# Layers 0 to 2 of a four-layer block: phases behind barriers against one interleaved order of attention and feed-forward steps

## The chip, the cores and the metric

The kernel runs on one core of one Trainium2 chip. The metric is the device time of one execution in microseconds; the median of three runs of the kernel before is 2029.81 us (2028.09 to 2031.36). Names of engines: PE is the matrix engine (TensorE), DVE is VectorE, ACT is ScalarE, POOL is GpSimd, SP issues most DMAs.

## The reference

Input x is (2, 1024, 256), a context is (2, 154, 256), and all arithmetic is float32. Four layers, each a cross-attention and a feed-forward part, both added to x after a layer norm:

```python
    x = x + _L0_xattn_ref(_layernorm(x, axis=-1), ctx_1024, ...)   # 16 heads of 16, softmax over 154 positions
    x = x + _L0_ffn_ref(_layernorm(x, axis=-1), ...)     # ternary weights 256->1024->256, relu squared
    x = x + _L1_xattn_ref(_layernorm(x, axis=-1), ctx_1024, ...)
    x = x + _L1_ffn_ref(_layernorm(x, axis=-1), ...)     # product keys: 4 heads x 8 of 4096 table rows, plus a gated MLP
    x = x + _L2_xattn_ref(_layernorm(x, axis=-1), ctx_1024, ...)   # with rotary positions
    x = x + _L2_ffn_ref(_layernorm(x, axis=-1), ...)     # 8 experts, 2 taken, plus a shared one; gate and up, then down
    x = x + _L3_xattn_ref(_layernorm(x, axis=-1), ctx_1024, ...)   # autocorrelation instead of softmax
    x = x + _L3_ffn_ref(_layernorm(x, axis=-1), ...)     # 8 linear experts, 2 taken
```

The part of layer 1 that matters most here: for each of the 2048 tokens, 32 rows of a table are fetched, each with a 256-wide half for a dot product with the normed token and a 256-wide half that is added to x, weighted:

```python
        de = down_embed[indices]
        ue = up_embed[indices]
        ew = jnp.einsum('btd,bthkd->bthk', hidden_states, de)
        ew = jax.nn.silu(ew) * jax.nn.softmax(scores, axis=-1)
        experts_states = jnp.einsum('bthk,bthkd->btd', ew, ue)
```

## The kernel before

Tokens are handled in 4 chunks of 512 (four tiles of 128 partitions). `schedule()` lists phases: the keys and values of a layer (`kv`), then for layer 0 the attention of all four chunks, the preparation of the ternary weights (`tern`) and the four feed-forward chunks; for layers 1 and 2 the attention and the feed-forward part of chunk 0, then of chunk 1, and so on; layer 3 follows. Every engine runs the phases in this order. A phase begins on each engine with `enter`, which waits until the other two compute engines have left the phase before, and ends with `leave` (a drain). Phases share one buffer (`bufA`) and all PSUM banks.

An attention chunk has these steps. In the first pass, 12 units of up to 6 heads (of 16 per tile) are multiplied on PE (L495) and their row maxima taken on DVE (L1199, L1202, L1203), with three pairs of PSUM banks. The maxima are turned on PE (L500), copied by ACT and sent by DMA as one more row of the queries. In the second pass, scores of 4 heads at a time go to PSUM (L523, L529), ACT takes the exponentials two heads at a time (L866, L868), PE weighs the values (L510, L513). Then the result is turned (L543), divided on DVE (L1222, L1223), turned again (L548) and projected (L553). The queries of the next chunk are projected ahead (`stack`: L454), cut into three bf16 parts on DVE (L1131 to L1133), written to DRAM, and read back by SP in another layout (L1577) once the second pass no longer needs the old ones.

The layer norm of the next phase is `front`: DVE takes statistics and, with a square root from ACT, normalises (L1108 to L1123), PE turns (L443), ACT copies. ffn0 has 8 hidden tiles (L597) and 4 output tiles (L606); ffn1 has the similarities and their top 8 (L624, L1285, L1289), gate and up (L634), the choice of the 32 rows of each token (`sums` to `prob`, L1298 to L1332) and the output (L652 onwards is ffn2's); ffn2 has 10 tiles of gate and up (L663, four matmuls each, in two alternating pairs of banks) and 36 output tiles (L675).

The gather of layer 1 is cut into 128 groups of 4 fetches, 32 groups for each chunk. POOL issues the fetches (L1539, 256 KB each) into a ring of `RING = 20` row buffers, which is five groups: group g waits until group g-5 has been added. DVE computes the dots (L1043), ACT a tanh (L817), DVE the weights (L1055, L1059) and the additions (L1048). A call for group g finishes group g-1: it holds the additions of g-1 between the dots of g. A table gives the places of the groups in the phases of layers 1 and 2, over all of them up to the third ffn2:

```python
STEPS = dict(kv=(2, 0, 4), attn1=(1, 3, 2, 0, 4, 0, 1), attn2=(0, 2, 3, 0, 2, 1, 1), ffn1=(2, 0, 0, 1, 0, 0, 2),
             ffn2=(2, (1, 1, 1, 0, 1, 1, 1, 1, 1, 0), 0, 4, 2))
```

Of the kernel before, what the change touches and what calls it, by code (L numbers as in the profile page):

```python
# [9 lines left out]
P = 128  # L18
STOP = None
B, T, D = 2, 1024, 256  # L20
S = 154
H, DH = 16, 16
KT = D // P
# [15 lines left out]
RING, GRP = 20, 4  # L39
NG = PH * TOPK // GRP  # L40

# [8 lines left out]


STEPS = dict(kv=(2, 0, 4), attn1=(1, 3, 2, 0, 4, 0, 1), attn2=(0, 2, 3, 0, 2, 1, 1), ffn1=(2, 0, 0, 1, 0, 0, 2),
             ffn2=(2, (1, 1, 1, 0, 1, 1, 1, 1, 1, 0), 0, 4, 2))

TERN_ROWS = {1: range(0, 4), 2: range(4, 8), 3: range(8, 10)}


ATTN_PACK = dict(wq=KT * D, wk=KT * D, wv=KT * D, wo=KT * D, bq=2, bk=2, bv=D, bo=D)
# [3 lines left out]
FFN2_PACK = dict(gate=KT * E2, gu=KT * M2 * 2 * P, down=M2 * D)  # L62
# [3 lines left out]
ROPE_PACK = dict(cos=T, sin=T)  # L66
# [9 lines left out]

def schedule():

    out = [("kv", 0, 0)] + [("attn", 0, c) for c in range(NCH)] + [("tern", 0, 0)]

    out += [("ffn0", 0, c) for c in range(NCH - 1)] + [("kv", 1, 0), ("ffn0", 0, NCH - 1)]
    for layer in (1, 2):
        for c in range(NCH):
            out.append(("attn", layer, c))
            if layer == 1 and c == NCH - 1:
                out.append(("kv", 2, 0))
            out.append((f"ffn{layer}", layer, c))  # L90
    out.append(("kv3", 3, 0))
    for b in range(B):
        out += [("q3", b, 2 * b), ("q3", b, 2 * b + 1), ("corr", b, 0)]
    out += [("out3", b, 0) for b in range(B)]
    out += [("ffn3", 3, c) for c in range(NCH)]
    return out


def build(nc, io, stop=None):
    phases = schedule()[:stop]  # L100
    fronts = [n for n, (kind, _, _) in enumerate(phases) if kind in ("attn", "ffn0", "ffn1", "ffn2", "q3", "ffn3")]
    front_of = {n: f for f, n in enumerate(fronts)}

    def instance(n):

        return sum(p[0] == phases[n][0] for p in phases[:n])

    def next_front(n):

        f = sum(m <= n for m in fronts)  # L110
        if f >= len(fronts):
            return None
        m = fronts[f]
        kind, b, _ = phases[n]
        if phases[m][0] == "ffn3" and phases[m - 1][0] == "out3":
            return f if kind == "out3" and b == 1 else None

        return f if n == (fronts[f - 1] if f else 0) else None

    def is_tail(n):  # L120

        f = next_front(n)
        return f is not None and phases[fronts[f]][2] == phases[n][2]

    def stack_of(n):

        return n + 1 if n + 1 < len(phases) and phases[n + 1][0] == "attn" else None

    def stacks_before(f):

        return sum(phases[m][0] == "attn" for m in fronts[:f])

    ctx = ExitStack()
    with ctx:
# [8 lines left out]
        xg = [sb(f"xg{i}", [P, TI, D]) for i in range(3)]  # L143
        xt = sb("xt", [P, KT, CH])
        stats = sb("stats", [P, TI, 6])
        mv = sb("mv", [P, TI, 2])
        vare, stdev, newton, rstd = (sb(s, [P, TI]) for s in ("vare", "stdev", "newton", "rstd"))
# [7 lines left out]
        RN, (LC, LN) = columns(ROPE_PACK)[1], columns(LATE_PACK)  # L155
        const = sb("const", [P, KN])
        ctxt = sb("ctxt", [P, KT, B * S])
        wattn = sb("wattn", [P, max(AN, CN)])
        wf = sb("wf", [P, max(4096, F1N, F2N, F3N)])
        bufA = sb("bufA", [P, 8832])  # L160
        bufB = sb("bufB", [P, 10240])
        ringb = sb("ring", [P, RING * 2 * D])
# [1604 lines left out]
```

## Time and profile before

| what | value |
|---|---|
| median of three runs | 2029.81 us |
| span of the profiled execution | 2025.4 us |
| what lies around the span (median less span) | 4.4 us |
| layers 0 to 2 | 0 to 1675 us |
| layer 3 | 1675 to 2025.4 us |
| PE, DVE, ACT, POOL busy, of the span | 69%, 62%, 20%, 26% |
| 128 groups of the gather | from 571 to about 1516 us |

The profiled execution has no device time of its own in the profile beside its span, so the difference to the median stands for what lies around it. Busy times of one engine's instructions overlap a little at their edges, so that a sum of durations is longer than the time in which they run; where it matters, start-to-start times are used.

### The profile page before, as it was taken

How to read it: one execution, taken by the hardware profiler on the slowest of the kernel's cores; microseconds unless marked ns; L12 is line 12 of the kernel's file. 1: busy time of each engine (PE TensorE's matmuls, PEld its weight loads, DVE VectorE, ACT ScalarE, POOL GpSimd, SP SyncE). 2: the span in 40 equal slices, each digit the busy share in tenths (PEclk: the TensorE clock that was granted, in tenths of full speed). 3: DMA queues.
4: the chain of work that ended last, by engine and by line, in shares of the span. 5: the costliest groups of instructions: out<-in, count | busy, mean ns of one | idle time of the engine just before them, and what ended most of it. 6: DMA issues, size and time to landing. Idle time of an engine off the chain costs nothing.

```text
span 2025.4 us, 16984 instructions
## 1 busy us (share of the span) xinstructions
PE 1400.9 (69%) x5070; PEld 728.6 (36%) x5070; DVE 1255.7 (62%) x4181; ACT 415.0 (20%) x711; POOL 533.8 (26%) x560
## 2 busy tenths in 40 slices
PE   4566689976736556465627657837737788898998
PEld 2233346543312323222313233323414354344544
DVE  3445533433858878886887888878877244321675
ACT  1323341113113122131204203212210411100110
POOL 1000000000057246254426745753740000011000
PEclk8777789988958867786857877867877899999999
DMA  6433300250198468558686996996863102120000
GB/s 137 116 37 53 52 26 1 29 92 12 31 188 185 90 147 193 102 140 194 133 192 174 193 166 154 191 187 120 195 138 52 44 0 68 34 66 27 11 11 21
DMA packets 101196, 202.63 MB, mean 100 GB/s; under 512 B 27568, under 2 KB 65328, under 8 KB 99952
## 3 DMA queue, kind: packets, MB, share of 16 engines
q0 software_dynamic: 40960, 134.25, 29.8%
q1 hardware_dynamic: 60144, 67.30, 17.9%
q8 instruction: 40, 0.66, 0.1%
q14 instruction: 52, 0.43, 0.1%
HBM read 185.58 MB, written 15.73 MB: 99 GB/s over the span
## 4 chain that ended last, share of the span: by engine, by line
PE 39%; DVE 26%; DMA 17%; POOL 7%; issue 5%; ACT 3%; SPq 1%; ACTq 0%; DVEq 0%
DMA bufB<-scr_queries 8%; POOL ring L1539 7%; DVE m L1199 5%; PE psum L693 4%; DMA ring<-in_table,rowid 3%; PE psum L752 3%; DVE x_sb L1048 3%; PE psum L597 3%; PE psum L763 3%; DMA scr_queries<-bufB 2%; PE psum L523 2%; DVE ring L1043 2%; PE psum L634 2%; PE psum L606 2%; PE psum L663 2%
## 5 line engine op out<-in xcount | busy, mean ns | idle before, releaser
L1539 POOL DMA_INDIRECT ring<-in_table,rowid x512 | 508.9, 994 | 764.5 <-DVE prob L1332 329.7
L495 PE MATMUL psum<-bufB 112*128 112x154 bf16 x768 | 109.5, 316 | 224.9 <-DMA bufB<-scr_queries 184.2
L1048 DVE SCALAR_TENSOR_TENSOR x_sb<-ring,ew,x_sb 128x256 f32<-128x256 f32 x512 | 246.5, 481 | 5.0
L1043 DVE CUSTOM_DVE_ANT_0 ring<-xg,ring 128x256 f32<-128x256 f32 x512 | 212.8, 416 | 13.8 <-DMA ring<-in_table,rowid 13.8
L495 PEld LDWEIGHTS psum<-bufB 112*128 112x128 bf16 x768 | 78.6, 132 | 257.3 <-issue 191.0
L1525 POOL TENSOR_TENSOR x_sb<-x_sb,wattn 128x256 f32<-128x256 f32 x32 | 22.0, 721 | 539.8 <-ACTq L276 286.9
L1199 DVE TENSOR_REDUCE m<-psum 128x6 f32<-128x924 f32 x96 | 103.0, 1115 | 86.9 <-PE psum L495 82.0
L663 PE MATMUL psum<-xt,wf 128*128 128x512 f32 x320 | 148.4, 619 | 10.2 <-DVE bufA L1354 9.0
L1127 DVE TENSOR_TENSOR x_sb<-x_sb,psum 128x256 f32<-128x256 f32 x128 | 50.3, 418 | 125.4 <-PE psum L606 45.6
L817 ACT ACTIVATE thalf<-dots 128x4 f32<-128x4 f32 x128 | 26.2, 205 | 452.8 <-DVE dots L1043 452.1
L693 PE MATMUL psum<-wf,xt 128*128 128x512 f32 x256 | 114.3, 603 | 1.1 <-DVE x_sb L1425 1.0
L675 PE MATMUL psum<-wf,bufA 128*128 128x256 f32 x320 | 84.3, 426 | 42.4 <-DVE x_sb L1365 42.4
L523 PE MATMUL psum<-bufB 113*128 113x512 bf16 x192 | 68.1, 486 | 46.1 <-DMA bufB<-mt 40.2
L866 ACT ACTIVATE bufA<-psum 128x1024 f32<-128x1024 f32 x96 | 93.2, 1029 | 31.6 <-PE psum L523 31.5
L443 PE MATMUL psum<-const,xa 128*128 128x128 f32 x224 | 39.2, 333 | 83.5 <-DVE xa L1123 83.5
L663 PEld LDWEIGHTS psum<-xt,wf 128*128 128x128 f32 x320 | 61.8, 198 | 93.7 <-issue 70.6
L675 PEld LDWEIGHTS psum<-wf,bufA 128*128 128x128 f32 x320 | 64.4, 212 | 63.2 <-DVE x_sb L1365 51.0
L1055 DVE SCALAR_TENSOR_TENSOR ew<-dots,prob 128x4 f32<-128x4 f32 x128 | 20.4, 159 | 99.2 <-ACT thalf L817 55.7
L1425 DVE SCALAR_TENSOR_TENSOR x_sb<-psum,bufA,x_sb 128x256 f32<-128x256 f32 x128 | 61.6, 484 | 31.6 <-PE psum L693 27.1
L763 PE MATMUL psum<-bufA,bufB 128*128 128x512 f32 x160 | 71.7, 610 | 5.8 <-DMA bufA<-scr_roll 4.6
L1365 DVE SCALAR_TENSOR_TENSOR x_sb<-psum,bufA,x_sb 128x256 f32<-128x256 f32 x128 | 61.8, 483 | 16.6 <-PE psum L675 5.3
L1108 DVE BATCH_NORM_STATS2 stats<-x_sb 128x6 f32<-128x256 f32 x128 | 44.9, 413 | 43.7 <-ACTq L276 36.5
(225 smaller groups left out, 2252.8 us busy)
## 6 DMA issues: line engine op xcount, KB each, us to landing
bufB<-scr_queries SPq DMA_DIRECT2D x84, 256.0 KB, 10.0
scr_queries<-bufB SPq DMA_DIRECT2D x12, 768.0 KB, 3.7
ring<-in_table,rowid POOLq DMA_INDIRECT x512, 5.8
wf<-in_ffn SPq DMA_DIRECT2D x1, 3848.0 KB, 21.9
wattn<-in_attn SPq DMA_DIRECT2D x3, 1282.0 KB, 7.6
bufB<-scr_keys SPq DMA_DIRECT2D x42, 80.0 KB, 5.2
ring<-in_ffn SPq DMA_DIRECT2D x1, 2696.5 KB, 22.2
bufA<-scr_roll SPq DMA_DIRECT2D x4, 592.0 KB
```

The source lines that it names most:

```text
L495: ins = mm(psum[:, pair + z, at:at + S], queries[0:MROW, h, i * P:(i + 1) * P], keys(b)[0:MROW, h, 0:S], start=True, stop=True)
L523: ins = mm(bank(2 * a + z), keys(b)[0:MROW + 1, 4 * G + 2 * a + z, 0:P], queries[0:MROW + 1, 4 * G + 2 * a + z, :], start=True, stop=True)
L663: ins = mm(bank(2 * (m % 2) + r), gu[:, kt, m, r, :], x[:, kt, :], start=kt == 0, stop=kt == KT - 1)
L675: ins = mm(psum[:, y % 5, 0:D], hm2[:, m, i * P:(i + 1) * P], down[:, m, :], start=m == ms[0], stop=m == ms[-1])
L693: ins = mm(bank(y % 4), x[:, kt, i * P:(i + 1) * P], w3("we")[:, kt, e * 512:(e + 1) * 512], start=kt == 0, stop=kt == KT - 1)
L763: ins = mm(bank(2 * g + N), vst(b, g)[:, u, :], roll(2 * b + g)[:, at:at + 512], start=u == 0, stop=u == U - 1)
L866: act(p[:, 2 * a:2 * a + 2, :], psum[:, 2 * a:2 * a + 2, :], ACT.Exp).then_inc(at_ex, 1)
L1043: return eng.tensor_tensor_reduce(row, xg[c % 3][:, i, :], row, 1.0, 0.0, ALU.mult, ALU.add, dots[:, g % 4, j:j + 1])
L1048: return stt(x, ring[:, GRP * (g % (RING // GRP)) + j, D:2 * D], ew[:, g % 4, j:j + 1], x, ALU.mult, ALU.add)
L1199: eng.reduce_max(m4[:, i, h0:h1].rearrange("p (a b) -> p a b", a=2), psum[:, pair:pair + 2, 0:3 * S].rearrange("p a (b s) -> p a b s", b=3 ...
L1365: ins = add_x(c, i, src) if e == 8 else stt(x_sb[:, c * TI + i, :], src, comb2[0][:, i, e:e + 1], x_sb[:, c * TI + i, :], ALU.mult, ALU.add)
L1539: eng.indirect_dma_start(ring[:, s * GRP + j, :], None, io["table"], bass.IndirectOffsetOnAxis(ap=rowid[c % 3][:, at + j:at + j + 1], axis ...
```

## The change

The phases of layers 0 to 2 are replaced by a list of small items, which each engine walks through; what an engine has no part in, it skips. There is no barrier until layer 3; every buffer has its own semaphores. In each of 13 slots the attention items of one chunk are interleaved with the feed-forward items of the chunk before, by weights written beside them. The list's items: `p1` is a unit of the first pass, `s` half a group of the second pass, `w` the weighing, `t`, `o`, `y` the way back, `N` and `X` the two parts of a layer norm (for attention "a" and feed-forward "f"), `Q` the projection of queries, `L` their load, `g` one group of the gather.

PSUM is split: banks 0 to 3 belong to attention (first pass: two pairs instead of three; second pass: two single banks, one for the rest, one for the values), 4 and 5 to norms, queries and keys, 6 and 7 to the feed-forward part. So ffn0 has two banks for hidden tiles instead of four, and gate and up of ffn1 and ffn2 use the one pair 6 and 7. Exponentials are taken one head at a time. Keys and values are made per batch. The normalising multiplication moves from DVE to ACT. Similarities of ffn1 use only the non-zero half of the keys. The ring has `RING = 12` buffers, which is three groups, and the 128 groups are spread over slots 6 to 9 alone, 32 in each, evenly by number of items. SBUF for weights, norms and probabilities is cut anew, so that both halves of a slot fit.

```diff
-RING, GRP = 20, 4
+RING, GRP = 12, 4
+SLOTS = RING // GRP
...
+def ffn_items(layer, c):
+    if layer == 0:
+        out = [(1.75, ("h0", c, m)) for m in range(8)] + [(3.4, ("y0", c, i)) for i in range(TI)]
+    elif layer == 1:
+        out = [(3.5, ("q1", c))]
+        for i in range(TI):
+            out += [(1.0, ("sm1", c, i)), (3.5, ("gu1", c, i))]
+        out += [(0.1, ("tk1", c))] + [(1.8, ("y1", c, i)) for i in range(TI)]
+    else:
+        out = [(1.5, ("lg2", c))] + [(3.5, ("gu2", c, m)) for m in range(M2)]
+        out += [(0.5, ("y2", c, i, e)) for i in range(TI) for e in range(9)]
+    return out
...
+GATHER_PER_SLOT = {6: 32, 7: 32, 8: 32, 9: 32}
+CUTS = (0.22, 0.34, 0.42, 0.66, 0.86)
...
+        if a:
+            first, scores, back = attention_items(*a)
+            items += merged(first[:3], rest)
+            if f:
+                items.append((1.5, ("X", "f") + f))
+            if nxt:
+                items.append((0.0, ("N", "a") + nxt))
...
+            items += merged(first[3:9], ffn[0])
+            if nxt:
+                items += [(1.5, ("X", "a") + nxt)] + ffn[1] + [(3.6, ("Q",) + nxt)]
...
+            items += first[9:] + ffn[2] + merged(scores, ffn[3])
...
+            items += merged(back, ffn[4])
+            items.append((0.0, ("N", "f") + a))
...
+        order = [x for _, x in items]
+        n = GATHER_PER_SLOT.get(s, 0)
+        for z in range(n):
+            at = [q for q, x in enumerate(order) if x[0] != "g"]
+            order.insert(at[(2 * z + 1) * len(at) // (2 * n)], ("g",))
...
+            def gate2(c, m):
+                if m == 0:
+                    eng.wait_ge(f2_sc, c + 1)
+                else:
+                    eng.wait_ge(f2_hm, M2 * c + m)
...
-                if g >= RING // GRP:
-                    eng.wait_ge(f1_acc, g - RING // GRP + 1)
+                if g >= SLOTS:
+                    eng.wait_ge(f1_acc, g - SLOTS + 1)
```

What stood on PE at the first pass of chunk 1 of layer 0 (L495 is the first pass, L500 turns the maxima, L523 and L529 are scores, L443 turns a normed chunk):

```order
L495 MATMUL psum<-bufB 128x154 x64
L500 MATMUL psum<-const,m 16x128 x4
L523 MATMUL psum<-bufB 128x512 x4
L529 MATMUL psum<-bufB 32x512 x4
L443 MATMUL psum<-const,xa 128x128 x8
```

What stands there now (L595 is the first pass, L704 a hidden tile of ffn0 for chunk 0 with two matmuls each, L545 turns a normed chunk, L555 projects the next queries, L603 turns the maxima):

```order
L595 MATMUL psum<-bufB 128x154 x10
L545 MATMUL psum<-const,xa 128x128 x8
L595 MATMUL psum<-bufB 128x154 x6
L704 MATMUL psum<-xtf,wf 128x512 x2
L595 MATMUL psum<-bufB 128x154 x6
L704 MATMUL psum<-xtf,wf 128x512 x2
L595 MATMUL psum<-bufB 128x154 x10
```

The feed-forward tiles, the two norms and the queries have moved between the units of the first pass, whose maxima DVE takes.

On ACT, in the second pass of chunk 3 of layer 1, before (L817 is the tanh of a group, L866 and L868 are exponentials, L858 unloads the values):

```order
L866 ACTIVATE bufA<-psum 128x1024 x2
L868 ACTIVATE bufA<-psum,const 128x512
L817 ACTIVATE thalf<-dots 128x4
L866 ACTIVATE bufA<-psum 128x1024 x2
L868 ACTIVATE bufA<-psum,const 128x512
L858 ACTIVATE bufA<-psum 128x512
L817 ACTIVATE thalf<-dots 128x4 x2
```

The same pass of the same chunk now (L915 is the tanh, L978 and L983 are exponentials, L987 unloads, L1019 is the silu of ffn1 for chunk 2):

```order
L983 ACTIVATE bufR<-psum,const 128x512
L1019 ACT_TABLE_LOAD
L1019 ACTIVATE bufR<-psum 128x512
L915 ACTIVATE thalf<-dots 128x4
L978 ACT_TABLE_LOAD
L978 ACTIVATE bufR<-psum 128x512 x2
L987 ACTIVATE bufR<-psum 128x512
L915 ACTIVATE thalf<-dots 128x4
L978 ACTIVATE bufR<-psum 128x512 x2
L983 ACTIVATE bufR<-psum,const 128x512
```

Silu stands between exponentials, with a load of a function table ahead of it and one behind it, and the tanh of a group stands behind every second or third item. In the whole program ACT has 94 table loads now and had 60.

## Rows read from the trace of the kernel before

**Rows 1.** Stages: length, busy PE, PEld, DVE, ACT, POOL, clock, DMA share, GB/s.
```profile
324.20:354.30 30.10, 28.93 (x104) 19.01 (x105) 11.05 (x29) 5.85 (x11) 0.00 (x0) 1.00 0.00 1
452.70:501.00 48.30, 34.60 (x188) 16.57 (x188) 18.67 (x42) 16.84 (x22) 0.00 (x0) 0.82 0.09 37
571.00:1516.00 945.00, 549.22 (x1996) 279.18 (x1996) 771.07 (x2916) 201.22 (x375) 497.39 (x501) 0.75 0.76 162
1600.00:1675.00 75.00, 63.90 (x192) 38.06 (x192) 33.04 (x100) 12.81 (x20) 0.00 (x0) 0.89 0.08 29
1675.00:2025.40 350.40, 323.05 (x888) 153.68 (x888) 160.49 (x443) 39.15 (x74) 10.98 (x16) 0.99 0.12 34
0.00:1675.00 1675.00, 1077.89 (x4182) 574.88 (x4182) 1095.24 (x3739) 375.86 (x637) 522.79 (x544) 0.79 0.55 114
```

**Rows 2.** Who waited for whom, 0 to 1675 us; total, times, longest.
```profile
POOL ring L1539 <- DVE x_sb L1048: 290.6, 38, 32.5
...
PE psum L495 <- DMA bufB<-scr_queries: 184.2, 11, 30.6
...
DVE ew L1055 <- ACT thalf L817: 55.7, 21, 8.7
...
DVE ew L1055 <- DMA ring<-in_table,rowid: 39.4, 24, 3.2
```

**Rows 3.** PE in order of time; start, us, line, tiles, idle before.
```profile
120.04 4.80 PE L495 MATMUL psum<-bufB 112*128 112x154 bf16 x32 [9.55 <-DMA bufB<-scr_queries]
...
133.32 1.02 PE L500 MATMUL psum<-const,m 128*16 128x128 f32 x4 [2.37 <-DVEq L1205]
137.31 1.86 PE L523 MATMUL psum<-bufB 113*128 113x512 bf16 x4 [2.96 <-DMA bufB<-mt]
...
145.10 3.70 PE L454 MATMUL psum<-xt,wattn 128*128 128x512 f32 x8
...
159.23 1.97 PE L543 MATMUL psum<-const,bufA 128*128 128x128 f32 x16
...
324.25 13.97 PE L597 MATMUL psum<-xt,wf 128*128 128x512 f32 x32 [0.61 <-DVEq L276]
...
1609.87 36.26 PE L663 MATMUL psum<-xt,wf 128*128 128x512 f32 x80
...
1653.68 20.50 PE L675 MATMUL psum<-wf,bufA 128*128 128x256 f32 x80
```

**Rows 4.** DVE's pieces: norm, top 8 of a tile, row choice first, split, choice rest.
```profile
504.90:508.10 3.20, 3.17 (x4) 1.52 (x5) 2.62 (x13) 0.21 (x1) 0.00 (x0) 0.50 0.02 5
514.20:518.20 4.00, 4.00 (x10) 1.71 (x9) 3.91 (x24) 0.00 (x0) 0.00 (x0) 1.00 0.01 2
536.30:543.40 7.10, 6.63 (x23) 4.36 (x24) 7.02 (x52) 4.32 (x7) 0.00 (x0) 1.00 0.00 0
543.40:546.50 3.10, 3.10 (x16) 2.74 (x15) 3.00 (x3) 0.00 (x0) 0.00 (x0) 1.00 0.01 3
546.50:555.80 9.30, 0.87 (x5) 0.42 (x3) 9.03 (x17) 0.00 (x0) 0.00 (x0) 0.78 0.79 151
```

**Rows 5.** One group on DVE, from its first to its last instruction.
```profile
592.60 0.16 DVE L1055 SCALAR_TENSOR_TENSOR ew<-dots,prob 128x4 f32<-128x4 f32 x1 [0.23 <-DVE m L1203]
...
594.93 1.00 DVE L1048 SCALAR_TENSOR_TENSOR x_sb<-ring,ew,x_sb 128x256 f32<-128x256 f32 x2
```

**Rows 6.** POOL's fetches of the group that this group let go: first and fourth.
```profile
596.20 0.95 POOL L1539 DMA_INDIRECT ring<-in_table,rowid  x1 [4.74 <-DVE x_sb L1048]
...
599.95 0.94 POOL L1539 DMA_INDIRECT ring<-in_table,rowid  x1 [0.30 <-issue]
```

**Rows 7.** Landing of those four fetches (L1539, 596 to 600.5 us).
```profile
DMA to landing us min/median/max: 4.6/5.0/5.2
```

**Rows 8.** ACT around a table load, in order of time.
```profile
135.07 1.28 ACT L828 ACT_TABLE_LOAD   x1
136.37 0.20 ACT L828 ACTIVATE stdev<-vare 128x4 f32<-128x4 f32 x1
```

More of the change, by code:

```diff
@@ L48 @@
 NU = len(MAX_UNITS)
[L52 to L58, printed above, removed]
+ATTN_PACK = dict(wk=KT * D, wv=KT * D, bk=2, bv=D, wq=KT * D, bq=2, wo=KT * D, bo=D)
 CORR_PACK = ATTN_PACK
@@ L99, in build, with attention_items @@
[L99 to L131, printed above, removed]
+def attention_items(layer, c):
+    first = [(0.8, ("p1", layer, c, u)) for u in range(NU)] + [(0.6, ("mt", layer, c))]
+    scores = []
+    for G in range(G4):
+        scores.append((0.9, ("s", layer, c, G, 0)))
+        if G:
+            scores.append((2.0, ("w", layer, c, G - 1)))
+        scores.append((1.2, ("s", layer, c, G, 1)))
+    scores.append((2.0, ("w", layer, c, G4 - 1)))
+    back = [(0.7, ("t", layer, c, G)) for G in range(G4)] + [(0.7, ("o", layer, c, g)) for g in range(2)]
+    back += [(1.2, ("y", layer, c, i)) for i in range(TI)]
+    return first, scores, back
@@ new lines, in merged @@
+def merged(a, b, lag=0.0):
+    ta, tb = sum(w for w, _ in a) or 1.0, sum(w for w, _ in b) or 1.0
+    out, i, j, da, db = [], 0, 0, 0.0, lag * tb / ta
+    while i < len(a) or j < len(b):
+        if j == len(b) or (i < len(a) and da / ta <= db / tb):
+            da += a[i][0]
+            out.append(a[i])
+            i += 1
+        else:
+            db += b[j][0] * (1 - lag / ta)
+            out.append(b[j])
+            j += 1
+    return out
+GATHER_PER_SLOT = {6: 32, 7: 32, 8: 32, 9: 32}
@@ L498, in attn, with turn_max @@
+            def turn_max(layer, c):
+                k = chunk(layer, c)
                 eng.wait_ge(at_mx, NU * (k + 1))
@@ L846, in attn @@
-            def attn(n, layer, c):
-                k = instance(n)
-                enter(eng, "act", n)
-                gather_steps(gather.take(STEPS[f"attn{layer or 1}"][0]))
+                if f:
+                    eng.wait_ge(fr_tp, KT * f)
+                stacks = sum(i[0] == "Q" for i in order[:place["N", tgt, layer, c]])
+                if stacks:
+                    eng.wait_ge(sk_p, stacks)
+                eng.wait_ge(fr_sc, f + 1)
+                for i in range(TI):
+                    act(normed(tgt, layer, c)[:, i, :], x_sb[:, c * TI + i, :], ACT.Identity, bias=shift[:, i:i + 1],
+                        scale=rstd[:, i:i + 1]).then_inc(fr_xn, 1)
@@ L1667, in _ @@
+            for item in order:
+                if item[0] in work:
+                    work[item[0]](*item[1:])
             eng.wait_ge(end_pool, 1)
```

1832 lines of the change are left out of this document (942 added, 890 removed).

## The prediction

> **What bounds the kernel now.** I read the busy times by stage first. Layers 0 to 2 take 1675 us, in which PE is busy for 1078 and DVE for 1095 [rows 1]: neither is full, and the phases take turns in being bound by one or the other. An ffn0 phase is PE alone (28.9 of 30.1 us), an ffn2 phase without gathers mostly PE (63.9 of 75), and the 945 us with the gather are DVE's (771, while PE has 549) [rows 1]. Layer 3 has 350 us, 323 of them PE [rows 1]; the change leaves its work alone. Then I read the waits: PE stood 184.2 us for the queries that come back from DRAM, the largest wait of PE on the path, while DVE in all those stages waited only 39.4 us for gathered rows and 55.7 for the tanh; POOL in turn waited 290.6 us for additions to free the ring [rows 2]. So the ring of five groups is nearly always ahead of DVE, and DVE with its order of work sets the pace there.
>
> **The parts that the change moves, without gathers.** A slot now has three stretches.
>
> The first pass is DVE's. Its 12 units took 133.32 - 120.04 = 13.3 us before, of which PE worked a good half; it waited 2.37 at their end for the last maxima [rows 3]. Two norms now stand between the units; one is 3.2 us up to its scale [rows 4], and with a shift and a wait for ACT's square root I take 4, so 8. The split of the queries is 3.1 [rows 4]. Six squares of ffn0 are 4, an estimate from 0.5 us for 256 columns (1.00 for two additions, [rows 5]). The projection of the next queries hangs on the norm of the same slot: PE turns it, two hidden tiles (3.5 us), then 3.7 for the projection [rows 3] and some 2.8 for its bias on ACT, with three units of maxima behind it in DVE's order. I put 7 us of idle DVE there. Sum 36.
>
> The second pass had 159.23 - 137.31 = 21.9 us with a norm and a projection in it; these 5 us go, and two or three feed-forward tiles come: a hidden tile is 13.97 / 8 = 1.75 us, an output tile under (28.93 - 13.97) / 4 = 3.7, I take 3.5 [rows 1, 3]. With the 4 us to turn and send the maxima (133.32 to 137.31) the stretch is 4 + 17 + 8.7 = 30. The way back is some 8 us and one output tile: 11.
>
> Slots 1 to 4 so take 36 + 30 + 11 = 77, and 6 more in each of the two that hold keys and values: 77 x 4 + 12 = 320. Start and slot 0 I take as 58 + 88 = 146: the first queries came at about 63 us before and now come some 5 us earlier with keys of one batch only, and slot 0 is 77 less its 20 us of ffn0 and norm, plus some 31 for the ternary weights, 16 of them on DVE between the maxima and 15 inside the second pass, where PE waits for them. That is 466 us for what was done at 501 before, the end of chunk 0's attention in layer 1 [rows 1]: the waits for queries are hidden, but the maxima and the feed-forward tiles of PE do not overlap as well as two full engines would.
>
> Slot 5 has ffn1. Four top-8 steps of 4.0 us stand in DVE's order, and PE's gate and up use the banks of the similarities, so they follow each other: 1 + 4.0 + 3.5 + 1.9 = 10.4, four times. The choice of rows is 7.1 + 9.3 = 16.4 us on DVE [rows 4] in front of the divisions for which PE waits. 77 + 16 + some 15 that the four chains stick out = 108. So the first group comes at 466 + 108 = 574 us, as before (571), with one attention chunk more done than before.
>
> Slots 10 to 12 have ffn2. Ten tiles of 36.26 / 10 = 3.6 us and 36 outputs of 20.5 / 36 = 0.57 [rows 3]; with one pair of banks instead of two each tile now waits for the silu and product of the one before: 3.6 + 1.4 = 5.0, where nothing stands between. Slot 12 is 50 + 21 + 8 for norm and logits + 11 for its routing and the drain = 90. Slot 10: attention's 77 - 13 for its ffn0 tiles = 64, plus 36 + 16 of ffn2 that do not fit beside maxima, and 6 for rotary queries: 122. Slot 11 has no next queries: 105. With 12 us at the end of slot 9 without groups: 329.
>
> **The ring.** This is the term that decides. One group holds DVE from 592.60 to 595.93, 3.3 us [rows 5]. POOL begins 0.27 us later, at 596.20, its fourth fetch at 599.95 [rows 6], and this lands 5.0 us later [rows 7]: at 604.95. From the end of one call to the rows for the call three groups on are 9.1 us, and that call adds 3.3. With three groups in the ring the call for group g may begin only when the fetches have landed that the call for g-2 let go. So any two calls in a row take at least 12.4 us, 6.2 for a group; with five groups it is 12.4 for four calls, and no limit, which agrees with POOL's idle 290.6 us [rows 2]. The order has 127 intervals between calls. With 3.3 us a call, 1.1 a unit of maxima, 4.5 a norm, 4.0 a top 8, 16.3 the choice of rows, 8.5 a rotary query chunk and 0.4 to 0.65 for the small ones they hold 687 us of DVE's work. But in the second pass DVE has little else, and calls stand side by side. In 63 disjoint pairs of intervals, 50 hold less than 12.4 us (461 in all), 13 hold more (221, the choices of rows above all). 50 x 12.4 + 221 + 3 = 844. Where also every overlapping pair must hold, each call's end carried to the next but one, it is 876. I take 876 for 574 to 1450. Before, the groups took 945 us, but with two and a half ffn2 phases beside them, where now there is half of one: it is the same pace with less of the other work done.
>
> Against the ring stands one rule. A fetch of 256 KB lands after 4.6 to 5.2 us in the trace [rows 7]. The Trainium skill (DMA: Bandwidth & Descriptors, section Anatomy of one DMA — SWDGE (gpsimd) path) fits 2.0 us plus the bytes at 436 GB/s, an estimate of 2.6 us here. By it a pair would take 10.0 us, the same sum 763, and the whole 2022; the trace disagrees, and its landing is used.
>
> Table loads on ACT: 34 more, each 136.37 - 135.07 = 1.3 us [rows 8], 44 us. ACT is busy 201 of 945 us [rows 1], so most hide; those between silu and exponential are in the 1.4 above. The Trainium skill (ScalarE: Activation LUTs, section What ACT_TABLE_LOAD costs) adds a drain and comes to 2.66 us, 90 in all; rows 8 show no room for that drain.
>
> **The sum.** 466 + 108 + 876 + 329 = 1779 us for layers 0 to 2 instead of 1675. With 350 for layer 3 the span is 2129, plus 4.4 around it 2134. I predict 2135 us, 5% slower than the median of 2029.81.
>
> **The rivals.**
>
> Faster: the ring does not bind. It decides alone at a pair of about 10.1 us, where 876 has become 770 and the sum 2029. For it: a group's four fetches may meet emptier queues than the median. Then the floor is DVE's 687 us and 2134 - 189 = 1945. Time 1945 to 2025. Against: the fetches measured here are such ones, after 4.74 us of idle POOL [rows 6, 7]. 0.17.
>
> More coupled: every engine is in order and each slot mixes four chains, so DVE's waits for gate and up, for norms and for tanh add to the ring's instead of hiding in them. The 13 loose pairs and the seven norms then cost some 5 us each, 100, and slots 1 to 4 and 10 to 12 gain nothing over 86 and 125: 2200 to 2260. PE's clock, 0.75 in the gather stage against 1.00 in ffn0's [rows 1], speaks for it. 0.21.
>
> No change: gain of the hidden query waits (184.2 us) and loss of the ring cancel, within 0.2% (about what a measurement of this kernel can tell from no change). 0.02.
>
> The forecast, a ring-bound gather of 820 to 920 us and the rest within 5% of its sum of 903: 2060 to 2200. 0.60.
>
> **How the numbers follow.** The range 2020 to 2215 takes the forecast's, the upper end of the first rival and the lower part of the second. Bounds of single costs: the pair of calls 10.0 to 14.0 us (763 to 960); the first part 430 to 500, slot 5 90 to 120, the tail 290 to 360. Faster 0.17, same 0.02, slower 0.81.
>
> **What would show it.** The profile after should have POOL waiting for additions before nearly every group and DVE waiting for fetched rows some 150 us or more instead of 39.4; DVE less busy in the gather stage than 771 of 945 although it is denser on paper; PE's wait for queries near zero; the first group near 574 us and the last near 1450; layer 3 at about 350. Wrong would be the forecast if the groups run at under 6 us each, or if slots 1 to 4 take under 70 us.

## The result and the profile after

The changed kernel takes 2279.86 us (median of four runs, 2276.9 to 2288.5), the kernel before 2030.59 us beside it: a ratio of 1.1224, 95% interval 1.1186 to 1.1263. It is slower by 249 us. The sum forecast 2134, so 146 us were missing in it, and the time lies above the range of 2020 to 2215.

Stages of the changed kernel, with the columns of [rows 1]: start and slot 0; slots 1 to 4 with the attention of chunk 0 of layer 1; the rest of slot 5 up to the first group; the stretch with the gather; the last slots; layer 3; all of layers 0 to 2.

```profile
0.00:146.00 146.00, 75.23 (x354) 40.72 (x354) 66.75 (x146) 39.87 (x72) 8.38 (x24) 0.71 0.50 114
146.00:473.00 327.00, 265.27 (x1252) 148.41 (x1252) 126.43 (x287) 122.47 (x220) 7.34 (x8) 0.92 0.28 42
473.00:608.00 135.00, 87.20 (x352) 46.50 (x353) 65.93 (x248) 38.69 (x64) 11.50 (x12) 0.77 0.28 61
608.00:1580.00 972.00, 396.25 (x1424) 204.13 (x1422) 674.42 (x2673) 186.16 (x379) 493.63 (x500) 0.66 0.60 153
1580.00:1912.00 332.00, 253.37 (x883) 125.08 (x883) 127.91 (x329) 89.73 (x136) 0.00 (x0) 0.92 0.07 13
1912.00:2274.50 362.50, 331.31 (x896) 157.84 (x896) 151.91 (x420) 55.05 (x104) 10.97 (x16) 0.96 0.11 33
0.00:1912.00 1912.00, 1077.32 (x4263) 564.84 (x4263) 1061.44 (x3679) 476.93 (x871) 520.85 (x544) 0.76 0.42 100
```

Against the terms of the prediction: 473 for 466, 135 for 108, 972 for 876, 332 for 329, 362.5 for 350. The stretch with the gather holds two thirds of the miss. In layers 0 to 2 PE is busy for the same 1077 us as before. In the stretch with the gather it is busy for 396 of 972 us, so it is far from full there; but its granted clock (1.00 is 2.4 GHz, 0.50 is 1.2 GHz, and a stretch shows the mean of the two) is 0.66 instead of 0.75, and where DVE and PE wait for each other in turn, a slower PE lengthens the chain (see below).

Waits in layers 0 to 2, to be laid beside [rows 2]:

```profile
POOL bufR L1572 <- DVE x_sb L1125: 338.1, 99, 15.5
...
PE psum L595 <- DVE m L1263: 201.8, 38, 16.4
...
DVE ew L1130 <- DMA bufR<-in_table,rowid: 183.1, 62, 15.2
...
PE psum L652 <- DVE bufR L1276: 159.8, 12, 45.3
...
DVE ew L1130 <- ACT thalf L915: 35.7, 13, 3.8
...
PE psum L595 <- DMA bufB<-scr_queries: 22.5, 3, 18.8
```

The queries cost PE 22.5 us instead of 184.2: the interleaving does hide their way through DRAM. In their place stand the waits between PE and DVE (maxima, L1263; divisions, L1276). POOL waited 38 times for an addition and now does so 99 times, 3.4 us in the mean instead of 7.6: the ring has no free buffer nearly always. What DVE itself waited for from 608 to 1580 us:

```profile
DVE ew L1130 <- DMA bufR<-in_table,rowid: 183.1, 62, 15.2
DVE ew L1130 <- ACT thalf L915: 35.7, 13, 3.8
DVE bufR L1341 <- ACT bufR L1019: 32.6, 10, 6.7
DVE bufR L1411 <- ACT bufR L1035: 14.6, 5, 6.7
```

The first line is the ring. The others are not: the tanh of the group before, the silu of ffn1 (L1019) and of ffn2 (L1035). With small ones that are not shown, the waits that are not for rows come to 102 us. DVE's time in these 972 us is then 674 of work, 183 of waits for rows, 102 of other waits, and 12 that the view puts down to nothing. How the ring paces DVE is seen where calls have little between them. Starts of three calls on DVE, then on POOL the first and the fourth fetch that the first of these calls let go, and the first fetch of the next:

```profile
1500.49 0.16 DVE L1130 SCALAR_TENSOR_TENSOR ew<-dots,prob 128x4 f32<-128x4 f32 x1 [2.06 <-DMA bufR<-in_table,rowid]
...
1505.79 0.16 DVE L1130 SCALAR_TENSOR_TENSOR ew<-dots,prob 128x4 f32<-128x4 f32 x1 [1.05 <-DMA bufR<-in_table,rowid]
...
1511.84 0.23 DVE L1130 SCALAR_TENSOR_TENSOR ew<-dots,prob 128x4 f32<-128x4 f32 x1 [2.34 <-DMA bufR<-in_table,rowid]
```
```profile
1504.09 0.94 POOL L1572 DMA_INDIRECT bufR<-in_table,rowid  x1 [1.46 <-DVE x_sb L1125]
...
1507.84 1.17 POOL L1572 DMA_INDIRECT bufR<-in_table,rowid  x1 [0.30 <-issue]
1509.38 0.94 POOL L1572 DMA_INDIRECT bufR<-in_table,rowid  x1 [0.38 <-DVE x_sb L1125]
```

The last addition of the call that starts at 1500.49 ends at 1503.8, its fourth fetch goes out at 1507.84 and lands some 4 us later, and the call that needs it starts at 1511.84: 11.4 us for two calls here, 11.3 to 12.1 for the steady pairs late in slot 9, where 12.4 was worked out with a landing of 5.0 us.

The longest waits for rows stand right behind another transfer. SP's seven loads of queries go out at 741.79, ahead of the fetches of the next group:

```profile
741.79 3.27 SPq L1655 DMA_DIRECT2D bufB<-scr_queries  x7
...
742.65 0.94 POOL L1572 DMA_INDIRECT bufR<-in_table,rowid  x1 [3.03 <-DVE x_sb L1125]
```
```profile
761.11 0.16 DVE L1130 SCALAR_TENSOR_TENSOR ew<-dots,prob 128x4 f32<-128x4 f32 x1 [15.17 <-DMA bufR<-in_table,rowid]
```

The fetches issued from 741 to 748 us, by the trace of that line:

```profile
DMA to landing us min/median/max: 14.3/14.3/14.3
```

The median of all is 4.2 us. With three groups in flight nothing is left to work on in the meantime. The same happens at the query loads of 980, 1236 and 1451 us, and these four places hold 15.2, 9.5, 14.4 and 10.9 us, 50 of the 183. That the loads delay the rows is read from the order of events at all four places; no run moved the loads.

### The profile page after: what moved, and what is told of

Its sections match the earlier page's. It is cut to its first block, busy times and chain, and to the rows that moved or that the text cites. A ratio compares the mean times of both kernels' runs of the same rounds, so it can differ in the third digit from the quotient of the medians.

```text
span 2274.5 us, 17574 instructions
## 1 busy us (share of the span) xinstructions
PE 1408.6 (62%) x5158; PEld 722.7 (32%) x5158; DVE 1213.4 (53%) x4099; ACT 532.0 (23%) x975; POOL 531.8 (23%) x560
## 3 DMA queue, kind: packets, MB, share of 16 engines
q0 software_dynamic: 40960, 134.25, 22.5%
## 4 chain that ended last, share of the span: by engine, by line
PE 26%; DVE 13%; DMA 6%; ACT 4%; POOL 3%; issue 3%; ACTq 0%; DVEq 0%; POOLq 0%
PE psum L771 6%; DMA bufR<-in_table,rowid 6%; PE psum L878 5%; POOL bufR L1572 3%; DVE x_sb L1125 3%; PE psum L847 3%; PE psum L835 3%; PE psum L781 3%; DVE bufR L1121 2%; DVE bufR L1411 1%; ACT bufR L1035 1%; DVE stats L1186 1%; PE psum L858 1%; PE psum L815 1%; ACT xa L936 1%
## 5 line engine op out<-in xcount | busy, mean ns | idle before, releaser
L1572 POOL DMA_INDIRECT bufR<-in_table,rowid x512 | 505.1, 987 | 811.4 <-DVE prob L1371 346.9
L1125 DVE SCALAR_TENSOR_TENSOR x_sb<-bufR,ew,x_sb 128x256 f32<-128x256 f32 x512 | 247.5, 483 | 4.7
L595 PE MATMUL psum<-bufB 112*128 112x154 bf16 x768 | 84.2, 258 | 257.1 <-DVE m L1263 201.8
L1121 DVE CUSTOM_DVE_ANT_0 bufR<-bufR 128x256 f32<-128x256 f32 x512 | 214.6, 420 | 0.0
L771 PE MATMUL psum<-xtf,wf 128*128 128x512 f32 x320 | 162.9, 656 | 67.9 <-DVE bufR L1411 34.2
L740 PE MATMUL psum<-xtf,wf 128*128 128x512 f32 x128 | 96.2, 920 | 131.0 <-DVE bufR L1336 131.0
L595 PEld LDWEIGHTS psum<-bufB 112*128 112x128 bf16 x768 | 63.1, 108 | 304.3 <-DVE m L1263 215.7
L781 PE MATMUL psum<-wf,bufR 128*128 128x256 f32 x320 | 108.1, 460 | 69.6 <-DVE x_sb L1420 65.2
L1130 DVE SCALAR_TENSOR_TENSOR ew<-dots,prob 128x4 f32<-128x4 f32 x128 | 20.6, 161 | 222.7 <-DMA bufR<-in_table,rowid 183.1
L915 ACT ACTIVATE thalf<-dots 128x4 f32<-128x4 f32 x128 | 26.2, 204 | 478.2 <-DVE dots L1121 477.9
L878 PE MATMUL psum<-wf,xtf 128*128 128x512 f32 x256 | 117.9, 618 | 1.0 <-DVE x_sb L1530 1.0
L978 ACT ACTIVATE bufR<-psum 128x512 f32<-128x512 f32 x192 | 104.7, 604 | 48.5 <-PE psum L615 48.2
L1263 DVE TENSOR_REDUCE m<-psum 128x6 f32<-128x924 f32 x96 | 105.4, 1113 | 17.3 <-PE psum L595 16.7
L771 PEld LDWEIGHTS psum<-xtf,wf 128*128 128x128 f32 x320 | 64.0, 210 | 152.3 <-issue 67.9
L740 PEld LDWEIGHTS psum<-xtf,wf 128*128 128x128 f32 x128 | 37.2, 306 | 181.8 <-DVE bufR L1336 136.5
L781 PEld LDWEIGHTS psum<-wf,bufR 128*128 128x128 f32 x320 | 60.4, 218 | 108.2 <-issue 101.0
L1530 DVE SCALAR_TENSOR_TENSOR x_sb<-psum,bufR,x_sb 128x256 f32<-128x256 f32 x128 | 61.7, 484 | 33.2 <-PE psum L878 29.1
```

What stands on the lines that cost most here:

```text
L595: ins = mm(psum[:, pair + z, at:at + S], queries[0:MROW, h, i * P:(i + 1) * P], keys(b)[0:MROW, h, 0:S], start=True, stop=True)
L740: ins = mm(bank(6 + r), w1(name)[:, kt, m * P:(m + 1) * P], xtf[:, kt, :], start=kt == 0, stop=kt == KT - 1)
L771: ins = mm(bank(6 + r), gu[:, m, kt, r, :], xtf[:, kt, :], start=kt == 0, stop=kt == KT - 1)
L781: ins = mm(psum[:, 6 + y % 2, 0:D], hm2[:, m, i * P:(i + 1) * P], w2("down", M2)[:, m, :], start=m == ms[0], stop=m == ms[-1])
L878: ins = mm(bank(y % 4), xtf[:, kt, i * P:(i + 1) * P], w3("we")[:, kt, e * 512:(e + 1) * 512], start=kt == 0, stop=kt == KT - 1)
L978: act(probs[h % 6], bank(j % 2), ACT.Exp).then_inc(at_ex, 1)
```

## The experiments

The theory that the prediction stood on, **ring**: three groups in flight instead of five cost what is lost. The rival, **coupling**: in the interleaved order each engine's waits for the others add to the ring's. Two groups of runs had a chip on which the kernel before itself took longer than its 2030 us elsewhere: 2116 us for a_half, b_half, a_spread and a_l3norm, and 2123 us for a_half6, a_hide12, b_row20 and the first run of a_hide16. They are read by their stages and with care, since these chips don't lengthen every kernel alike. a_hide16 was run on one of them and on another chip, and took 80 us more on the slower one, 70 of them in slots 6 to 9 (868 us from the first pass of slot 6 to that of slot 10, against 798). The changed kernel's layers 0 to 2 took 1918 us on the other slower chip (a_l3norm) against 1912.

### What the ring costs, and what the rest costs

Four groups in flight (a_ring16):

```diff
-RING, GRP = 12, 4
+RING, GRP = 16, 4
-        bufR = sb("bufR", [P, R_XG + 3 * TI * D])
+        bufR = sb("bufR", [P, R_XG + 2 * TI * D])
```

> The changed kernel with 16 row buffers, four groups in flight, instead of 12. Room is made by two buffers instead of three for the normed copy, the probabilities and the row numbers; so that one is free in time, two or three calls more stand at the end of slots 6 and 7. Ring theory: DVE waited 183 us for fetched rows with three groups. The call intervals without these waits, carried on with 12.4 us over three calls instead of two, give 797 us for the 966 between first and last call, and the whole 2110 us (2095 to 2130); waits for rows on DVE under 30 us. Coupling theory: DVE meets, where it waited for rows, the tanh, the silu and the square root of other chains instead; half of the 183 us comes back there, 2190 us or more, and DVE's waits for gate, up and tanh rise from about 90 to 150 or more.

Measured 2170.98 us, 1.0694 of before (1.0662 to 1.0727): 109 us back, outside both expectations. The coupling theory's form, that DVE would meet other waits in place of the rows, fails: its waits for tanh and silu stayed as they were (35.4 us for the tanh, 35.7 before), and the time fell by about as much as the waits for rows did, which went from 183 to 77. But these 77 us are more than the 14 us that the pace of a ring of four should leave (797 us expected less the 783 without waits for rows); the longest, 11.8, 7.8 and 7.5 us, come right behind query loads.

Three groups in the old order (b_ring12), 12 of its 20 buffers in use:

```diff
-RING, GRP = 20, 4
+RING, GRP = 12, 4
```

> The kernel before with three groups in flight (12 of its 20 row buffers in use), its order untouched. Ring theory: its own intervals between calls without waits for rows (898 us), carried on with at least 12.4 us for any two calls, give 1052 instead of 936 us, so 2030 + 116 = 2146 us; with 12.0 for a pair 2132. DVE's waits for rows rise from 39 to about 150 us. Coupling theory (the ring itself costs little, the interleaving does): under 2080 us, since the phases have slack that takes up a late fetch.

2129.86 us, 1.0491 (1.0461 to 1.0521): the small ring costs 100 us in the old order too, near the 102 that the expectation had for pairs of 12.0 us. DVE's waits for rows went from 39.4 to 163.0 us.

Both orders without the gather (a_nogather, b_nogather): no fetch, dot, tanh or addition.

> The changed kernel without the gather of ffn1: no fetches, dots, tanh or added rows, so that output misses that part; everything else in its order. Slots 6 to 9 then are like slots 5 and 10 (135 and 142 us), so about 1860 us (1830 to 1890). Ring theory (the rest of the interleaved order is at least as good as before): not slower than the kernel before without its gather. Coupling theory: slower than it by 40 us or more, since the top-8 steps, gate and up, and the ffn2 tiles on one pair of banks follow each other.

> The kernel before without the gather of ffn1 in the same way (its output misses that part). Of 936 us between first and last call, the calls hold DVE for 128 x 3.3 = 422 and wait 39 for rows; PE was busy for 549 of 945 us there. If DVE was the bound all along, 2030 - 460 = 1570 us; if PE's phases and the hand-overs take its place, about 1700. Ring theory: not faster than the changed kernel without gather. Coupling theory: faster than it by 40 us or more.

1844.19 and 1835.05 us. The old order without its gather was expected at 1570 or 1700 us; both were far too low. Taking 415 us of work from DVE gave back 195, so DVE alone didn't bound that stretch. Everything else in the new order (hidden queries, shared banks, table loads, layer 3) costs 9 us net. The gather costs 2280 - 1844 = 436 us in the new order and 2030 - 1835 = 195 in the old one. The change's loss lies in this difference of 241 us, and the 109 us that a fourth group gives back are not quite half of it.

### A finer ring

Each buffer is given back by its own addition (a_row12), and the same with 16 buffers (a_row16):

```diff
-                if g >= SLOTS:
-                    eng.wait_ge(f1_acc, g - SLOTS + 1)
                 for j in range(GRP):
+                    if g >= SLOTS:
+                        eng.wait_ge(f1_acc, GRP * (g - SLOTS) + j + 1)
```

> The changed kernel with 12 row buffers as it is, but each buffer is given back to POOL by its own addition instead of all four by the last of the group. In a call the first addition ends 1.3 us after the start and the last 3.3, so the fetch loop of a pair of calls shrinks from 12.0 to 12.4 us to about 10.0, which is also what POOL needs for eight fetches at 1.25. Ring theory: the intervals without waits for rows, carried on with 10 us for any two calls, give 857 instead of 966 us, so about 2175 us (2155 to 2195), as much as a fourth group gave. Coupling theory or a ring that is bound by landing and not by the buffers: above 2230 us.

> Four groups in flight and row by row release together (the edits of the two kernels). Ring theory with its loop at 10 us over three calls: nothing of the ring is left but POOL's 5.0 us for a group, so 783 to 800 us between first and last call and 2110 us. If the 77 us that DVE still waited for rows with four groups come from late landings (behind the query loads of the same slot) and not from late release, little changes: 2150 us.

2222.82 us, 57 less than the changed kernel (expected 105 less, or 50 at most by the other theory), and 2162.08 us, 118 less (expected 2110 or 2150). Four buffers more and the finer release do not add up: 109 and 57 give 118 together. What is left of waits for rows in a_row16 is 56 us.

### Single couplings

The choice of rows moved behind the attention's divisions (a_tk), and tanh in place of silu (a_tanh):

```diff
-        out += [(0.1, ("tk1", c))] + [(1.8, ("y1", c, i)) for i in range(TI)]
+        out += [(1.8, ("y1", c, 0)), (0.1, ("tk1", c))] + [(1.8, ("y1", c, i)) for i in range(1, TI)]
...
-                act(sg1, bank(6), ACT.Silu).then_inc(f1_sg, 1)
+                act(sg1, bank(6), ACT.Tanh).then_inc(f1_sg, 1)
```

> The changed kernel with the choice of rows (16.3 us on DVE) moved in each of slots 5 to 8 from ahead of the attention's divisions to behind them and the first output tile of the feed-forward part. Coupling theory: PE waited 15 us in slot 5 for the divisions behind it, so slot 5 and the way back of slots 6 to 8 get shorter, 15 us in slot 5 and up to 10 in each of the other three: about 2245 us. Ring theory: only slot 5 gets shorter, since DVE or the ring sets the pace in the others and has the same work: 2265 us. The fetch of a chunk begins some 12 us later, which nothing waits for at this point.

> The changed kernel with tanh in place of silu in ffn1 and ffn2, a function that the half tanh of the gather uses too (the output is another one): same work, without most of the table loads between silu, exponential and tanh (25 to 40 loads of 1.28 us). Coupling theory: the loads stand between PE's gate and the product on DVE in 56 tiles and cost on the path, 40 us less: 2240 us. Otherwise ACT's loads are hidden: 2270 to 2280 us.

2287.51 us for a_tk, 8 more where both theories had less: slot 5 got 8 us shorter, but DVE waited 203 us for rows instead of 183. The expectation said that nothing waits for the later fetch; that was wrong for chunk 0, whose first call waited 3.5 us. The fetches of the later chunks waited for buffers and not for the choice of rows, as before, so that the other 17 us, spread over slots 6 to 9, are not explained. a_tanh (whose output is another one) has 49 table loads instead of 94 and takes 2271.28 us, 9 less: that is 0.2 us for a load of 1.28, so nearly all of them are hidden.

### Room, and the place of the calls

Half of the gather, two rows in each group (a_half, b_half; the latter from `RING, GRP = 20, 4` to `10, 2`), and in the new order once more with six such groups in flight (a_half6). The first line of each edit:

```diff
-RING, GRP = 12, 4
+RING, GRP = 6, 2
```
```diff
-RING, GRP = 12, 4
+RING, GRP = 12, 2
```

> The changed kernel with half of the gather: two rows in each of the 128 groups instead of four, three groups in flight, every call at its place (its output misses half of the gathered rows). Full, the gather costs 436 us over the same order without it (2280 to 1844). Room theory: DVE is idle 275 of the 535 us of slots 6 to 9 without gather, so half of its 422 us of calls find room there and the cost is far under one half: 100 us or less, 1945 at most. Theory of the plain sum (each call adds its own time and its wait wherever it stands): 218 us, 2060.

> The kernel before with half of the gather in the same way (five groups of two rows in flight; its output misses half of the rows). Full it costs 195 us over the same order without gather (2030 to 1835). Room theory: in the old order the groups stand beside some 750 us of other work, in which DVE is busy for about 350; 211 us of calls fit, 1865 us or less. Plain sum: 98 us, 1933.

> The changed kernel with two rows in each of the 128 groups (half of the gathered rows are missing in the output) and six such groups in flight instead of three: the 97 us for which DVE still waited for rows in that form go. Room theory: slots 6 to 9 take 535 us without gather, 744 with half of it and a small ring; without the waits for rows 650 or less, the whole 1965. Plain sum (each call's time adds to the chain it stands in): 744 less only a part, 720 and 2035.

2060.28, 1883.34 and 1991.81 us. a_half came out at the 2060 of the plain sum, but DVE still waited 97 us for rows in it, so that it could not decide; in a_half6 it waited for none. Slots 6 to 9 of a_nogather, a_half6, and of a_row16 and a_hide16 as run together (below):

```profile
608.70:1143.80 535.10, 350.61 (x1396) 178.29 (x1397) 260.10 (x881) 146.08 (x235) 0.00 (x0) 0.78 0.19 33
```
```profile
609.10:1283.20 674.10, 371.49 (x1400) 189.78 (x1398) 476.79 (x1884) 180.71 (x372) 236.86 (x244) 0.73 0.48 121
```
```profile
606.00:1449.00 843.00, 383.09 (x1396) 196.58 (x1394) 662.94 (x2638) 183.76 (x376) 489.02 (x496) 0.69 0.72 176
```
```profile
607.70:1421.00 813.30, 381.42 (x1397) 195.08 (x1398) 661.97 (x2639) 179.42 (x370) 493.84 (x496) 0.70 0.74 182
```

Without gather DVE is idle for 275 of 535 us. Half of the gather adds 217 us to its busy time, which would all fit, and lengthens the four slots by 139. By these numbers a third of the calls' time is hidden and two thirds lengthen the chain, between the theory of room and the plain sum. But a_half6 ran on a slower chip and a_nogather did not, so that two thirds is an upper bound. A reason may lie in the form of the idle time. DVE's longest waits in those slots without gather, in the new order and (500 to 1400 us) in the old:

```profile
DVE bufR L1339 <- ACT bufR L1020: 76.8, 12, 7.4
DVE bufR L1409 <- ACT bufR L1036: 49.7, 10, 9.7
DVE bufR L1330 <- PE psum L733: 46.1, 9, 7.2
```
```profile
DVE bufA L1220 <- PE psum L544: 155.1, 7, 22.9
```

Most of the new order's idle time (173 of 275 us) is pieces of 5 to 7 us, each directly ahead of a product of gate and up or of a top-8 step, inside a chain that goes on at PE as soon as DVE has done it. The old order's longest are stretches of 22 us, one for each second pass, in which six calls of 3.3 us fit one behind the other. A piece of 5 to 7 us is long enough for a call too, but only for one that stands just there. In the old order half of the gather costs 1883 - 1835 = 48 us at most, since b_half had the slower chip.

The groups of each chunk spread over more of the program (a_spread, on a_row12): the next chunk's norm and queries come later in layer 2.

```diff
-GATHER_PER_SLOT = {6: 32, 7: 32, 8: 32, 9: 32}
+GATHER_PER_SLOT = {6: 29, 7: 29, 8: 29, 9: 28, 10: 15}
```

> On the kernel with row by row release and 12 buffers (2223 us): in layer 2 the norm, transposes and projection of the next chunk move from the middle of the maxima behind them and into the second pass (the transposed copy gets a place of its own for that), so that the groups of a chunk have until there: 29, 29, 29, 28 groups in slots 6 to 9 and 13 in the first part of slot 10, instead of 32 in each of four. Room theory: 13 groups move to where DVE has room, at 5.5 us each less what they now hide, so 40 us less, 2185 (2165 to 2205). If the groups cost the same wherever they stand: 2220 to 2235, the more as the queries now come later.

2238.31 us, against 2222.82 of a_row12 on another chip: the 40 us do not show. With no partner on its own chip, a slower one, it decides nothing.

The calls placed directly ahead of those waits (a_hide16, on a_row16; a_hide12, on the changed kernel):

```diff
+ROOM = {"gu1": 2, "sm1": 1, "gu2": 1, "kv": 2, "y": 1, "Q": 1}
...
-        for z in range(n):
-            at = [q for q, x in enumerate(order) if x[0] != "g"]
-            order.insert(at[(2 * z + 1) * len(at) // (2 * n)], ("g",))
+        if n:
+            order = beside_waits(order, n)
```

> On the kernel with 16 buffers and row by row release (2162 us): the same 32 groups per slot, but two directly ahead of each product of ffn1's gate and up, one ahead of each top-8 step, each product of ffn2, the keys' copy and the queries, and only the rest evenly. Without gather DVE waits 5.6 to 7.3 us ahead of each of those products, 7.1 ahead of two top-8 steps, 9.5 at the keys. Theory of place: some 17 calls of a slot (56 of 106 us) then lie in waits instead of lengthening the chain between PE and DVE; a slot goes from 210 to 185 us and the whole to 2070 (2050 to 2100). Theory that DVE is simply full or the rows are late: 2150 to 2170, with more waiting for rows where calls stand side by side.

> The same placing on the changed kernel itself, with its ring of three groups. Ring theory: any two calls still take 12.0 us, so that placing gives little or nothing: 2260 to 2290. Theory of place: 60 us or more less, 2220.

2208.42 and 2261.62 us, on the chip on which the kernel before took 2123. a_hide12 is where the ring theory had it, a_hide16 outside both expectations, and neither had a partner there. So a_row16 and a_hide16 were run as a pair.

> The kernel with 16 buffers and row by row release once more, as the partner of the next one on the same chip. It took 2162 us where the kernel before takes 2030.

> The kernel with the calls placed ahead of DVE's waits once more, now beside its partner. Theory of place: 60 us or more faster than a_row16_b. In the run on the other chip the waits for rows had gone, but the waits for the tanh had grown from 37 to 92 us, since a call's additions need the tanh of the group before, which ACT gives only after the exponentials and silus that stand ahead of it: by that theory (the wait changes its name) it is within 15 us of a_row16_b or slower.

2162.14 and 2128.32 us, 1.0655 (1.0625 to 1.0685) and 1.0490 (1.0463 to 1.0517) of before: the place of the calls is worth 34 us, between the two expectations. DVE's waits in those slots, first a_row16_b, then a_hide16_b:

```profile
DVE ew L1135 <- DMA bufR<-in_table,rowid: 56.0, 27, 7.2
DVE ew L1135 <- ACT thalf L915: 34.5, 17, 3.8
DVE bufR L1349 <- ACT bufR L1024: 33.2, 9, 7.3
```
```profile
DVE ew L1150 <- ACT thalf L930: 81.8, 28, 12.2
DVE ew L1150 <- DMA bufR<-in_table,rowid: 25.1, 12, 8.3
```

The waits for silu are filled (33 us before, 2 now) and those for rows halved, but the wait for the tanh has grown by 47 us, the larger part of what is missing to the 92 us of the theory. A call adds the rows of the group before, whose tanh stands in ACT's order behind exponentials and silus, the very ones that the call is placed beside.

### The rest

Layer 3's normalising multiplication on DVE again (a_l3norm), and the finer release in the kernel before (b_row20):

```diff
+                if layer == 3:
+                    eng.wait_ge(fr_tp, KT * f)
+                    eng.sem_inc(fr_sc, 1)
+                    for i in range(TI):
+                        ts(xa[:, i, :], x_sb[:, c * TI + i, :], mv[:, i, 0:1], rstd[:, i:i + 1], ALU.subtract, ALU.mult)\
+                            .then_inc(fr_xn, 1)
+                    return
```

> The changed kernel with the normalising multiplication of layer 3 on DVE as before the change (1.4 us for four tiles instead of 1.12 of wait and 2.07 on ACT), all else the same. Layer 3 took 362.5 us instead of 350. If that is the ACT norm, with its wait in front of the transposes of out3 and q3, 8 norms by 1.8 us where they are on the path: 8 to 12 us less, 2270. If it is the colder start of layer 3 (PE's first matmuls took 4.24 instead of 2.31 us) and the later evacuations: 3 us or less.

> The kernel before with row by row release and its five groups. DVE waited 39 us for rows in it. If those are late releases, 10 to 25 us less: 2005 to 2020, faster than either kernel. If they are the first rows of a chunk and late landings, no change: 2025 to 2032.

a_l3norm took 2275.15 us; its layer 3:

```profile
1918.10:2275.00 356.90, 328.66 (x896) 156.78 (x896) 160.50 (x441) 40.67 (x76) 11.03 (x16) 0.97 0.11 34
```

356.9 for 362.5 us: some 6 of the 12.5 us are the norm on ACT, between the two expectations, and the other half is not. b_row20 took 2138.05 us where the kernel before took 2123.44 (1.0063, 1.0040 to 1.0087): with five groups in flight a finer release gains nothing, the 10 to 25 us of the one theory are not there.

No version with the whole gather beats the kernel before. The best of the new order, a_hide16_b, is 97 us behind it.

## Why the prediction was wrong

**The direction and the ring: right, the size of the ring's wait partly by luck.** The three-group ring was worked out as 876 - 687 = 189 us of waiting on DVE; it waited 183.1. But a steady pair of calls takes 11.3 to 12.1 us where 12.4 was said, and the 50 us behind the query loads, which the prediction did not have, make up for it: two errors that cancel. That the ring costs time is shown: a fourth group gives 109 us back, and a small ring costs 100 in the old order, by itself. The Trainium skill (DMA: Bandwidth & Descriptors, section Anatomy of one DMA — SWDGE (gpsimd) path), with a fixed 2.0 us and the bytes at 436 GB/s, gives an estimate of 2.6 us for a landing; the changed kernel's rows take 3.2 us at least and 4.2 in the median, so the trace disagrees here too.

**The step that failed** is "Where also every overlapping pair must hold, each call's end carried to the next but one, it is 876". It takes the larger of the ring's pace and DVE's own work of 687 us, and so assumes that DVE waits for nothing but rows. It had 674 us of work, 183 of waiting for rows, 102 more for silu (47), tanh (36) and small things, and 12 that no wait explains: together 972. These waits did not hide in the ring's, as a_ring16 shows: there the waits for rows went down by 106 us, the others stayed, and the time fell by 109. That was the rival "more coupled". It was named with a chance of 0.21, but priced as 13 pairs and seven norms, 5 us each; the chain of similarities, top 8, gate, silu and product in slots 6 to 8 and the tiles of ffn2 in slot 9 were not in the price, although the prediction had the same chain in its term for slot 5.

**Slot 5: 108 forecast, 135 measured.** DVE waited 25.6 us for the silu and 15.7 for the similarities, and PE 15.4 us for the divisions behind the choice of rows:

```profile
586.24 2.36 PE L652 MATMUL psum<-const,bufR 128*128 128x128 f32 x8 [15.39 <-DVE bufR L1276]
```

"Some 15 that the four chains stick out" was the mis-sized term; with 77 and 16 as they stood they stick out by some 40. Moving the choice of rows (a_tk) gives 8 us of the slot. Some 10 more are in the 3.5 us for gate and up of one tile: the same eight matmuls, first in the kernel before, then in the changed one, took

```profile
520.87 3.60 PE L634 MATMUL psum<-xt,wf 128*128 128x512 f32 x8
```
```profile
493.43 5.87 PE L740 MATMUL psum<-xtf,wf 128*128 128x512 f32 x8 [3.54 <-DVE bufR L1336]
```

and the four tiles of slot 5 took 5.9, 6.1, 5.1 and 6.6 us, at granted clocks of 0.55 to 0.72 where it was 1.00 before; each stood behind a wait of PE for DVE's top 8 of 3 to 5 us. In the 12 us ahead of the first tile PE had been busy for 11.1 us in the kernel before, and for 5.8 of 11.4 in the changed one. The tiles of slots 6 to 8 are as slow, with the gather (924 ns a matmul) and without it (910 in a_nogather; 599 in the kernel before). So the prediction took its matmul times from a place where PE is busier and its granted clock higher, and missed a part of the coupling's price. No run changes the clock alone, so that what it costs on the path is not measured.

**Slots 1 to 4: 77 forecast, 83 with keys and values, 80 to 86 measured; the tail 329 and 332.** Right within 7 us for the four slots and 3 for the tail. The hidden queries are real.

**"The change leaves its work alone"** of layer 3: 12.5 us wrong. Its norms had moved to ACT, 2.07 us behind a wait of 1.12 instead of 1.38 on DVE; half of the miss is that (a_l3norm), the cause of the other half stays open.

**The comparison of gather stages** said "it is the same pace with less of the other work done", and had the size of the loss there but not its cause. Of the 241 us that the gather costs more in the new order, 118 are the ring (a_row16) and 34 the place of the calls (a_hide16_b). For the remaining 89 there is a sum from the stages, and no run that shows it alone: without gather the four slots are 535 us long, and with it DVE has 662 us of work in them, 127 more than they are long. In the old order the groups stood over 945 us; less the 195 that the gather costs there, that is a stretch of 750 us, into which 771 us of DVE's work went, 21 more. So the four slots are too short for the groups by 106 us more than the old stretch was, and DVE's idle time beside its work (151 of 813 us, against 174 of 945) takes 23 of that back, which leaves 83 of the 89. Waits for the tanh (82 us) are a part of these 151 that a call with the tanh one group further back might take away, and PE at the lower clock is another (its matmuls in the four slots take 351 us without gather at a clock of 0.78, and 381 at 0.70 with it); neither was tried.

**The range** ended at 2215 because each bound was moved alone (a pair of 10 to 14 us, 763 to 960 for the stretch). The waits beside the ring belonged to the upper bound of the same term.

## What to carry to other kernels

Before a third chain goes between two others, compare the work of the in-order engine that all three share with the length of the stretch: here 662 us of DVE's work went into slots that were 535 us long. Where it would fit, as half of the gather did, take the idle time apart by what ends it, and put the calls in front of those waits; calls spread evenly found at least a third of their time there and not all of it, and placing them gave 34 us of a hoped 92, since they then met a wait of their own, the tanh. A ring sized by its average pace must also bridge the longest landing, here 14 us behind another queue's loads. Matmul times read where PE is busy are too short for a place where it waits in between. And where a forecast takes the larger of two limits, look for the waits that belong to neither and add them.

## What was not expected of the hardware

Rows fetched behind SP's seven query loads land after 10.8 to 14.3 us instead of 4.2, at four places of the changed kernel. Of 45 table loads taken away, 58 us of ACT's time, 9 us came back. The kernel before takes 2024 to 2041 us on most chips and 2099 to 2143 on two others; the changed kernel's layers 0 to 2 took 1918 us on one of these two against 1912. Of the 80 us that a_hide16 took more on the other of the two, 70 lie in the slots with the gather and 5 ahead of them. What differs between the chips the traces here do not settle.
